# A layer norm and routing stage begun four tiles at a time, projections in token halves, and row scores by deadline

## The chip, the cores and the metric

The kernel runs on one core of one Trainium2 chip. The metric is the device time of one execution in microseconds. Before the change it is 1077.17 us, the median of 3 runs (1075.95 to 1077.93). The engines are named as the profile names them: PE (TensorE, its weight loads as PEld), DVE (VectorE), ACT (ScalarE), POOL (GpSimd) and SP (SyncE), which issues nearly all transfers. About 0.2% (2 us) is what a measurement of this kernel can tell from no change.

## The reference

`x` is 2 sequences of 1024 tokens with 128 features. Three parts follow each other: a mixture of experts, an attention, and the same mixture again.

```python
x = x + 0.5 * ffn(layernorm(x))
x = x + attn(layernorm(x))
x = x + 0.5 * ffn(layernorm(x))

def attn(x):                      # 16 heads, latent width 64, head width 8
    q = (x @ Wq + bq); k = (x @ Wk + bk); v = (x @ Wv + bv)
    qc = einsum('bthd,dl->bthl', q, Wc)
    att = softmax(causal(einsum('bthl,bshl->bhts', qc, k) / 8))
    return einsum('bhts,bshl->bthl', att, v) @ Wo + bo

def ffn(x):                       # 32 experts in 8 groups, top 4, capacity 320
    shared = silu(x @ sg) * (x @ su) @ sd
    # best 4 of 8 groups by cosine, best 4 experts among them, softmax gates,
    # each token's place within an expert by a running count, over 320 dropped
    buf = scatter(x);  h = silu(buf @ wg) * (buf @ wu);  out = h @ wd
    return shared + gathered_and_weighted(out)
```

## The kernel before, in words

The program is written engine by engine, with semaphores between them; nothing schedules it, so each engine's order is the order of the code. Tokens are 16 tiles of 128; `HT` = 8 tiles are one half, H (one sequence).

**First mixture.** `ln(0, 0)` on DVE takes the statistics of eight tiles (L847, L850), ACT the roots (L640), DVE the normalised rows (L861); PE transposes them (L1180), ACT copies them to `xnT` (L646), PE scores them against the centroids (L1188), and DVE routes them four tiles at a time (`route_steps`, from L871). When the slots of four tiles are known (L944), POOL scatters their rows to the expert buffers in HBM, one indirect transfer for each tile and choice (L552): 64 of them in a row, and the experts wait for the last. Ahead of all this DVE clears several buffers and normalises the centroids, whose transpose PE makes first (L1412). The expert loop follows, then `results` (SP, L452) loads each tile's four result rows and `combine` (DVE, L1034) adds them.

**Attention.** `ln(2, 0)` normalises the first sequence. Then four projections (`J`: q and k, each for tokens 0 to 511 and 512 to 1023; PE L1323) are split by ACT (L696, the high part) and DVE (L1046, the low part) and stored in `qkbuf` in HBM, three row blocks each (SP L476, `projected`). `group_in` loads the rows of four heads back, 4 transfers to `Qx` and 4 to `Kz`. There are 8 groups of heads (4 for each sequence), each with 4 chunks of 256 queries (a *unit*), and each unit has 4, 8, 12 or 16 *steps*: a step is one key tile for two heads. A step on PE is the transposed scores (L1356, `s_cols`), exp on ACT (L752), for the tiles on the diagonal a mask on POOL (L568), and three steps later the product with the values (L1375, `pv`).

The exp needs each row's maximum, which is added in the matmul, so the scores are computed twice. The first pass is the *row items* (`R`: PE L1331 and, on the diagonal, L1334; DVE L1052 takes the maximum). After the last `R` of a unit DVE makes the maxima ready (`max_parts`, L1061 to L1063), and a `T` item lets PE transpose them (L1342) and DVE add them to `Qx` (L1070). A unit's first step waits for its `T`. All row items use two banks in turn, so PE waits for DVE with every item but one. `ROW_STEP` says behind which step a row item stands, on PE, DVE and SP alike. In the kernel before it follows from `LEAD`: the items of a group run from step 6 of the group before it, evenly over 40 steps. There are 363 row items: 40 ahead of the first step (`EARLY`), 183 beside the 160 steps of the first sequence and 140 beside the 160 of the second, the last at step 285. The value tiles (L1290, ACT L734) of the first sequence stand between the projections and the early items.

When a unit ends, ACT copies sums (L705) and results, DVE inverts the sums (L1096), SP spreads them over the partitions with 8 transfers (L499, `spread_sums`), and POOL scales the unit (L588).

## Time and profile before

| | |
|---|---|
| median of 3 runs | 1077.17 us |
| profiled execution | 1078.49 us |
| its span | 1076.7 us |
| scatter of the first mixture, POOL | 31.8 to 112.6 us |
| expert loop | 113 to 256 us |
| from the loop's end to the first row item | 256 to 300.7 us |
| early row items | 300.7 to 328.6 us |
| steps of the first sequence, PE | 328.6 to 566 us |
| steps of the second sequence, PE | 608 to 832 us |
| second scatter, routing and second expert loop | to 1076.7 us |

The span runs from the first to the last instruction; the profiled execution's own time is 1.8 us more. A start time in a row below is counted from the beginning of the span.

### The profile page before, as it was taken

The numbers are of one execution on the slowest core, as the hardware profiler recorded it, in microseconds if no ns is written. First come the engines' busy times: TensorE is split into PE (matmuls) and PEld (weight loads), VectorE is DVE, ScalarE is ACT, GpSimd is POOL, SyncE is SP. The second block draws the span as 40 slices with busy tenths as digits, with TensorE's granted clock in tenths as the row PEclk, the third lists the DMA queues.
The fourth block names the chain that finished last, engine by engine and source line by source line (L and its number), as shares of the span: only waits on it lengthen the run. The fifth ranks groups of instructions, "written<-read, shape, count | busy, mean of one in ns | idle before, by whom it ended". The sixth has DMA issues, their size and how long they took to land.

```text
span 1076.7 us, 16412 instructions
## 1 busy us (share of the span) xinstructions
PE 873.8 (81%) x5041; PEld 720.3 (67%) x5041; DVE 567.6 (53%) x1624; ACT 406.9 (38%) x803; POOL 399.4 (37%) x583
## 2 busy tenths in 40 slices
PE   2358599992678998998999799899999845899993
PEld 1235477771246887987888488888888823687773
DVE  6743245444369665665752575566641362345444
ACT  2101132321314564554641454656566211233323
POOL 2677266654002222221210111354642046356651
PEclk9999699997789999999999899999999868899997
DMA  9510345553620011114101001112110100446536
GB/s 357 205 49 25 104 145 177 172 153 118 196 53 1 20 43 30 43 41 139 30 21 42 1 10 34 42 51 60 47 34 21 40 21 25 146 138 190 167 105 198
DMA packets 96245, 94.11 MB, mean 87 GB/s; under 512 B 15274, under 2 KB 83004, under 8 KB 95415
## 3 DMA queue, kind: packets, MB, share of 16 engines
q1 hardware_dynamic: 86966, 81.00, 25.1%
q0 software_dynamic: 9216, 12.33, 3.7%
q8 instruction: 33, 0.54, 0.2%
q14 instruction: 30, 0.24, 0.1%
HBM read 54.95 MB, written 37.03 MB: 85 GB/s over the span
## 4 chain that ended last, share of the span: by engine, by line
PE 52%; DVE 15%; POOL 10%; SPq 7%; DMA 7%; issue 7%; ACT 1%; POOLq 0%; DVEq 0%; ACTq 0%
PE PS L1375 15%; PE PS L1282 8%; POOL xbuf L552 7%; PE PS L1269 6%; SPq L499 6%; PE PS L1331 5%; PE PS L1270 5%; PE PS L1356 4%; PE PS L1406 3%; DVE mxp L1052 3%; DVE den L1096 2%; DMA rden<-den 2%; DVE xs L1034 2%; PE PS L1243 2%; POOL area_o L588 2%
## 5 line engine op out<-in xcount | busy, mean ns | idle before, releaser
L1375 PE MATMUL PS<-pT,area_v 128*128 128x256 f32 (+1 forms) x1280 | 307.7, 364 | 20.4 <-POOL pT L568 20.2
L1052 DVE TENSOR_REDUCE mxp<-PS 128x2 f32<-128x512 f32 (+1 forms) x320 | 197.7, 630 | 149.5 <-PE PS L1331 81.9
L752 ACT ACTIVATE pT<-PS 128x512 f32<-128x512 f32 (+1 forms) x320 | 176.7, 554 | 186.7 <-PE PS L1356 183.9
L1375 PEld LDWEIGHTS PS<-pT,area_v 128*128 128x128 f32 x1280 | 211.7, 192 | 36.8 <-issue 22.5
L602 POOL DMA_INDIRECT ybuf<-area_o,yidx x160 | 155.6, 973 | 128.5 <-DVE area_o L1008 89.5
L1331 PE MATMUL PS<-Kz,Qx 128*128 128x256 f32 (+1 forms) x640 | 169.0, 355 | 17.5 <-DVE mxp L1052 11.1
L552 POOL DMA_INDIRECT xbuf<-xn,sidx x128 | 125.4, 980 | 88.3 <-issue 62.0
L1356 PE MATMUL PS<-Qx,Kz 128*128 128x256 f32 (+1 forms) x640 | 142.7, 305 | 6.6 <-ACT pT L752 5.5
L1331 PEld LDWEIGHTS PS<-Kz,Qx 128*128 128x128 f32 x640 | 113.6, 196 | 39.0 <-DVE mxp L1052 19.6
L588 POOL TENSOR_TENSOR area_o<-area_o,rden 128x512 f32<-128x512 f32 x32 | 40.7, 1271 | 258.5 <-DMA rden<-den 258.5
L568 POOL TENSOR_SCALAR_AFFINE_SELECT pT<-pT 128x128 f32<-128x128 f32 x256 | 67.7, 299 | 178.9 <-ACT pT L752 178.6
L685 ACT ACTIVATE area_o<-PS 128x320 f32<-128x320 f32 x128 | 56.0, 437 | 147.0 <-PE PS L1270 138.0
L1356 PEld LDWEIGHTS PS<-Qx,Kz 128*128 128x128 f32 x640 | 102.0, 194 | 11.8 <-ACT pT L752 7.2
L1000 DVE TENSOR_TENSOR area_o<-area_o,PS 128x320 f32<-128x320 f32 x128 | 62.3, 488 | 79.2 <-ACT area_o L685 75.1
L1269 PE MATMUL PS<-area_o,area_v 128*128 128x320 f32 x256 | 96.1, 458 | 6.5 <-DVE area_o L1000 4.3
L1282 PEld LDWEIGHTS PS<-area_v,area_o 128*128 128x128 f32 x768 | 93.3, 192 | 5.3
L1282 PE MATMUL PS<-area_v,area_o 128*128 128x128 f32 x768 | 96.2, 275 | 0.0
L1270 PE MATMUL PS<-area_o,area_v 128*128 128x320 f32 x256 | 92.1, 442 | 0.0
L1096 DVE RECIPROCAL den<-den 128x128 f32<-128x128 f32 x64 | 59.4, 936 | 37.2 <-ACT den L705 37.2
L1269 PEld LDWEIGHTS PS<-area_o,area_v 128*128 128x128 f32 x256 | 44.7, 196 | 34.6 <-DVE area_o L1000 23.5
L1270 PEld LDWEIGHTS PS<-area_o,area_v 128*128 128x128 f32 x256 | 49.9, 195 | 21.3 <-issue 1.8
L705 ACT ACTIVATE den<-PS 32x256 f32<-32x256 f32 x128 | 47.9, 374 | 8.5 <-PE PS L1375 6.0
(160 smaller groups left out, 859.2 us busy)
## 6 DMA issues: line engine op xcount, KB each, us to landing
area_v<-xbuf SPq DMA_DIRECT2D x32, 340.0 KB, 3.2
area_v<-in_L_ffn_wg_dram SPq DMA_DIRECT2D x32, 256.0 KB, 3.4
area_v<-in_L_ffn_wu_dram SPq DMA_DIRECT2D x32, 256.0 KB, 3.7
area_v<-in_L_ffn_wd_dram SPq DMA_DIRECT2D x64, 128.0 KB, 2.5
rden<-den SPq DMA_DIRECT2D x256, 32.0 KB, 1.8
yg<-ybuf SPq DMA_DIRECT2D x24, 256.0 KB, 4.3
qkbuf<-stage SPq DMA_DIRECT2D x24, 256.0 KB, 3.0
xbuf<-Kz SPq DMA_DIRECT2D x4, 1360.0 KB, 10.9
```

What stands on the lines that cost most here:

```text
L552: pool.indirect_dma_start(xbuf[:, :], bass.IndirectOffsetOnAxis(ap=sidx[:, H, t * K + k:t * K + k + 1], axis=0), xn[:, H * HT + t, :], Non ...
L568: ins = nc.gpsimd.affine_select(out=block_, in_=block_, pattern=[[1, P]], compare_op=ALU.is_ge, fill=zero, base=0, channel_multiplier=-1)
L602: pool.indirect_dma_start(ybuf[:, :], bass.IndirectOffsetOnAxis(ap=yidx[:, j, t:t + 1], axis=0), yo[j][:, t, :], None, bounds_check=RES - ...
L752: nc.scalar.activation(pT[:, N % 4, 0:w], PS[:, 2 + N % 2, 0:w], ACT.Exp).then_inc(exp_done, 1)
L1052: nc.vector.tensor_reduce(mxp[:, i, c, 2 * hp:2 * hp + 2], PS[:, k % 2, 0:2 * w].rearrange("p (h w) -> p h w", h=2), AX.X, ALU.max).then_i ...
L1096: ins = nc.vector.reciprocal(part, part)
L1269: mm(PS[:, 2 + c, 0:CAP], wgt[j][:, a, c * P:(c + 1) * P], rhs, start=True, stop=True)
L1270: mm(PS[:, 4 + c, 0:CAP], wut[j][:, a, c * P:(c + 1) * P], rhs, start=True, stop=True)\
L1282: ins = mm(PS[:, bank, slot * D:(slot + 1) * D], hp[:, c, t * P:(t + 1) * P], wdt[j][:, a, c, :], start=(first and c == 0), stop=(c == HC ...
L1331: ins = mm(PS[:, k % 2, hh * w:(hh + 1) * w], Qx[Gi % 2][:, i * P:(i + 1) * P], Kz[Gi % 2][:, 2 * hp + hh, TC * c:TC * c + w], start=(hh = ...
L1356: ins = mm(PS[:, 2 + N % 2, a * w:(a + 1) * w], Kz[Gi % 2][:, 2 * p + a, j * P:(j + 1) * P], Qx[Gi % 2][:, t1 - w:t1], start=(a == 0), sto ...
L1375: ins = mm(PS[:, pv_bank(U, a), (p + 1) * TC - w:(p + 1) * TC], value_and_ones(j, h), pT[:, N % 4, a * w:(a + 1) * w], start=(first and p ...
```

## The change

It has five parts.

1. *First tiles by themselves.* The first four tiles of `x` are the first transfer, and `ln_first` does statistics, roots and normalised rows for four tiles, then the centroids (their squares now on DVE instead of ACT), then the second four tiles, and last the casts of the constants, which stood ahead of everything. PE scores tiles 0 to 3 before it transposes tiles 4 to 7. POOL clears only `Kz0` at the start and `Kz1` behind its 64 scatters.
2. *Token halves.* Combine, layer norm and transposes between the expert loop and the attention go in halves of four tiles. The projections go in the order q and k of tokens 0 to 511, then q and k of 512 to 1023. Between the halves stand four value tiles.
3. *Loads.* In `qkbuf` each head has 32 rows (8 of constants and 24 of data) instead of 26, so one transfer brings q for all four heads, and four bring k: 5 instead of 8 for a group, now called a visit. The first visit is loaded in two halves of 512 tokens. The constants are written early, behind the zeroing.
4. *Row scores by deadline.* 18 row items stand ahead of the first step, those of units 0 and 1 with the four projections. Each later visit's items end two steps before its last unit begins: 188 beside the first sequence's steps, 157 beside the second's, the last at step 301. The `T` of a visit's last unit stands directly behind that unit's last `R`, no longer three items later.
5. The second half's combine moves from steps 2 to 8 to steps 20 to 32; the 32 scatters within the second sequence stand on consecutive steps without a mask from step 210.

```diff
-R0 = 2
-RQ = R0 + 3 * HD
+R0 = RW - 3 * HD
...
+COMB_STEPS = (20, 24, 28, 32)
+SCAT_STEPS = [n for n in range(FIRST[V_C] + 10, len(STEPS)) if n not in DIAG][:K * HT]
+
...
+    for U, (vu, c) in enumerate(UNITS):
+        if vu == v:
+            pieces = [("R", i, k, min(TC, (i + 1) * P - k * TC), hp, (i, k, hp) == (2 * c + 1, c, 1))
+                      for i in (2 * c, 2 * c + 1) for k in range(c + 1) for hp in range(2)]
+            if U > 2 and UNITS[U - 1][0] == v:
+                pieces.insert(3, ("T", U - 1))
+            items += pieces
+            if U < 2 or c == VISITS[v][2][-1]:
+                items.append(("T", U))
+    if v == 0:
+        items = [("J", 0, q, h) for h in range(2) for q in range(2)] + items
...
+    if v == V_J:
+        items[14:14] = [("J", 1, q, h) for h in range(2) for q in range(2)]
...
+ROW_ITEMS = [(v, item) for v in range(len(VISITS)) for item in row_items(v)]
+ROW_NUMBER = {item if item[0] != "R" else (v, item): k for k, (v, item) in enumerate(ROW_ITEMS)}
+N_EARLY = ROW_NUMBER[("T", 1)] + 1
...
+def row_steps():
+
+    steps, end = [-1] * N_EARLY, 0
+    for v, visit in enumerate(VISITS):
+        mine = [k for k, (vk, item) in enumerate(ROW_ITEMS) if vk == v and k >= N_EARLY]
+        last = max(UNIT_FIRST[U] for U, (vu, c) in enumerate(UNITS) if vu == v) - 2
+        begin = 0 if v == 0 else max(end, FIRST[v - 1] + 3)
+        steps += [begin + i * (last - begin) // len(mine) for i in range(len(mine))]
+        end = last
...
+ROW_STEP = row_steps()
...
-EARLY = [k for k, s in enumerate(ROW_STEP) if s < 0]
...
+            def x_in_part(h):
+                sp.dma_start(xs[:, 4 * h:4 * h + 4, :], x_t[:, 4 * h:4 * h + 4, :]).then_inc(s_x[h], 16)
+
+            x_in_part(0)
             sp.dma_start(cst[:], consts).then_inc(s_const, 16)
-            for h in range(4):
-                sp.dma_start(xs[:, 4 * h:4 * h + 4, :], x_t[:, 4 * h:4 * h + 4, :]).then_inc(s_x, 16)
             sp.dma_start(cen[0:G, :], gcen).then_inc(s_cen, 16)
             sp.dma_start(cen[G:G + E, :], ecen).then_inc(s_cen, 16)
             sp.dma_start(ebb[:], ebias.partition_broadcast(P)).then_inc(s_cen, 16)
+            for h in range(1, 4):
+                x_in_part(h)
...
+            for b in range(B):
+                sp.dma_start(qkbuf[b, 0, :, 0:R0, :], Kz[0][:, 1, :].bitcast(F32)).then_inc(qk_const, 16)
+                sp.dma_start(qkbuf[b, 1, :, 2:R0, :], Kz[0][0:(R0 - 2) * NH, 1, :].bitcast(F32)).then_inc(qk_const, 16)
+                sp.dma_start(qkbuf[b, 1, :, 0:2, :],
+                             rden[0][0:4 * NH].rearrange("p a t -> p (a t)")).then_inc(qk_const, 16)
...
-            def group_in(Gi):
-
-                b, g = Gi // NG, Gi % NG
-                for j in range(2):
-                    sp.wait_ge(qk_out[j], 16 * 6 * (b + 1))
-                if Gi >= 2:
-                    sp.wait_ge(st_ready, SLOT * (Gi - 1))
+            def visit_in(v, cols, arrived):
+
+                b, g, chunks = VISITS[v]
+                heads = qkbuf[b, :, HG * g:HG * g + HG, :, cols]
+                sp.dma_start(Qx[v % 2][:, cols].bitcast(F32), heads[0].rearrange("h r t -> (h r) t")).then_inc(arrived, 16)
                 for hh in range(HG):
-                    rows = slice(RW * hh, RW * hh + RQ)
-                    sp.dma_start(Qx[Gi % 2][rows, :].bitcast(F32), qkbuf[b, 0, HG * g + hh]).then_inc(qk_in[Gi % 2], 16)
-                    sp.dma_start(Kz[Gi % 2][rows, hh, :].bitcast(F32), qkbuf[b, 1, HG * g + hh]).then_inc(qk_in[Gi % 2], 16)
+                    sp.dma_start(Kz[v % 2][RW * hh:RW * hh + RW, hh, cols].bitcast(F32), heads[1, hh]).then_inc(arrived, 16)
...
-            for k in range(4):
-                projected(k)
...
-            group_in(0)
-            group_in(1)
...
+            for h in range(2):
+                for k in range(2 * h, 2 * h + 2):
+                    projected(k)
+                if h == 0:
+                    sp.wait_ge(qk_const, 16 * 6)
+                    sp.wait_ge(s_zero1, 1)
+                    sp.wait_ge(s_fill, 64)
+                    sp.wait_ge(s_filly, 32)
+                for j in range(2):
+                    sp.wait_ge(qk_out[j], 16 * 3 * (h + 1))
+                visit_in(0, slice(512 * h, 512 * h + 512), (qk_half, qk_in[0])[h])
+            visit_in(1, slice(0, T), qk_in[1])
...
+                if step in FIRST[1:-1]:
+                    v = FIRST.index(step) + 1
...
+                    sp.wait_ge(st_ready, step)
+                    visit_in(v, slice(0, T), qk_in[v % 2])
...
+            zero_k(0, s_zero)
...
+            zero_k(1, s_zero1)
...
+            for h in range(2):
+                ln_std_dev(2, h)
+                ln_scaled(2, 0, (h,))
+                for k in range(2 * h, 2 * h + 2):
+                    high_part(k)
+                if h == 0:
+                    values(0, range(HT // 2))
+            load_table(ACT.Exp)
+            values(0, range(HT // 2, HT))
+            heads(0)
+            values(1, range(HT))
+            heads(1)
...
+            def ln_half(h):
+                ln_stats(0, *LN_FIRST[h])
+                ln_spread(2, h, *LN_FIRST[h])
+                ln_rows(2, 0, h, *LN_FIRST[h])
...
+            def ln_first():
+                dve.wait_ge(s_x[0], 16)
+                ln_stats(0, *LN_FIRST[0])
+                ln_spread(0, 0, *LN_FIRST[0])
+                ln_rows(0, 0, 0, *LN_FIRST[0])
+                centroid_squares()
+                dve.wait_ge(s_x[1], 16)
+                ln_stats(0, *LN_FIRST[1])
+                centroids()
+                ln_spread(0, 1, *LN_FIRST[1])
+                halves()
+                ln_rows(0, 0, 1, *LN_FIRST[1])
+                dve.wait_ge(s_ct, 1)
+                nc.vector.tensor_copy(cenT[:], PS[:, 6, 0:G + E]).then_inc(s_ctc, 1)
...
-                    inverses(step, b)
-                out_rows(b)
+            combine_part(0, 0, 0, 4)
+            dve.wait_ge(comb, 4)
+            ln_half(0)
+            combine_part(0, 0, 4, 4)
+            for k in range(2):
+                row_item(k)
+            dve.wait_ge(comb, HT)
+            ln_half(1)
+            for k in range(2, N_EARLY):
+                row_item(k)
...
+            for h in range(2):
+                ln_half(2, 0, h)
+                pe.wait_ge(xnT_ready, 5 + h)
+                for k in range(2 * h, 2 * h + 2):
+                    row_item(k)
+                if h == 0:
+                    for j in range(HT // 2):
+                        value_tile(0, j)
+            for i, k in enumerate(range(4, N_EARLY)):
+                row_item(k)
+                if i < HT:
+                    value_half(0, HT // 2 + i // 2, i % 2)
+            pe.wait_ge(v_a, HT)
+            pe.wait_ge(v_ones, 1)
```

Order on DVE from the first statistics on. `st`, `mv`, `rstd`, `rn` and `xn` are the layer norm, `csq` and `pT` the centroids, `yg` the routing's work space. Before:

```order
L826 TENSOR_SCALAR csq<-csq 40x1
L827 RECIPROCAL csq<-csq 40x1
L828 TENSOR_SCALAR pT<-pT,csq 40x128
L830 COPY cenT<-PS 128x40
L847 BN_STATS st<-xs 128x6 x8
L850 BN_AGGR mv<-st 128x2 x8
L853 RECIPROCAL rstd<-std 128x8
L855 TENSOR_TENSOR rn<-dev,rstd 128x8
L856 TENSOR_SCALAR rn<-rn 128x8
L857 RECIPROCAL rn<-rn 128x8
L861 TENSOR_SCALAR xn<-xs,mv,rstd 128x128 x8
```

and now:

```order
L899 BN_STATS st<-xs 128x6 x4
L904 BN_AGGR mv<-st 128x2 x4
L909 RECIPROCAL rstd<-std 128x4
L911 TENSOR_TENSOR rn<-dev,rstd 128x4
L912 TENSOR_SCALAR rn<-rn 128x4
L913 RECIPROCAL rn<-rn 128x4
L917 TENSOR_SCALAR xn<-xs,mv,rstd 128x128 x4
L867 TENSOR_TENSOR pT<-pT 40x128
L868 TENSOR_REDUCE csq<-pT 40x1
L899 BN_STATS st<-xs 128x6 x4
L872 TENSOR_SCALAR csq<-csq 40x1
```

The normalised rows of four tiles now come ahead of the centroids, which came first before.

Order on PE behind the first expert loop: transposes (`cst,xn`), projections (`xnT,wq` and `xnT,wk`), value tiles (`wv_in,xnT`) and row items (`Kz,Qx`). Before:

```order
L1180 MATMUL PS<-cst,xn 128x128 x8
L1323 MATMUL PS<-xnT,wq 128x512 x2
L1323 MATMUL PS<-xnT,wk 128x512 x2
L1290 MATMUL PS<-wv_in,xnT 128x512 x8
L1331 MATMUL PS<-Kz,Qx 128x128 x2
L1334 MATMUL PS<-causS,identb 128x256
L1331 MATMUL PS<-Kz,Qx 128x128 x2
L1334 MATMUL PS<-causS,identb 128x256
```

and now:

```order
L1259 MATMUL PS<-cst,xn 128x128 x4
L1402 MATMUL PS<-xnT,wq 128x512
L1402 MATMUL PS<-xnT,wk 128x512
L1369 MATMUL PS<-wv_in,xnT 128x512 x8
L1259 MATMUL PS<-cst,xn 128x128 x4
L1402 MATMUL PS<-xnT,wq 128x512
L1402 MATMUL PS<-xnT,wk 128x512
L1413 MATMUL PS<-Kz,Qx 128x128 x2
L1416 MATMUL PS<-causS,identb 128x256
L1369 MATMUL PS<-wv_in,xnT 128x512
L1413 MATMUL PS<-Kz,Qx 128x128 x2
L1416 MATMUL PS<-causS,identb 128x256
```

Two projections now stand behind four transposes, and four value tiles stand between the two halves.

Order on SP at the same place: result rows (`yg`), stores of the projections (`stage`) and loads. Before:

```order
L452 DMA yg<-ybuf 128x512 x16
L464 DMA qkbuf<-Kz 16x2x1024
L465 DMA qkbuf<-rden 16x4x512
L464 DMA qkbuf<-Kz 16x2x1024
L465 DMA qkbuf<-rden 16x4x512
L476 DMA qkbuf<-stage 16x8x512 x12
L488 DMA Qx<-qkbuf 26x1024
L489 DMA Kz<-qkbuf 26x1024
L488 DMA Qx<-qkbuf 26x1024
L489 DMA Kz<-qkbuf 26x1024
```

and now:

```order
L489 DMA yg<-ybuf 128x512 x16
L505 DMA qkbuf<-stage 16x8x512 x6
L512 DMA Qx<-qkbuf 128x512
L514 DMA Kz<-qkbuf 32x512 x4
L505 DMA qkbuf<-stage 16x8x512 x6
L512 DMA Qx<-qkbuf 128x512
L514 DMA Kz<-qkbuf 32x512 x4
L512 DMA Qx<-qkbuf 128x1024
L514 DMA Kz<-qkbuf 32x1024 x4
```

The first loads stand behind six stores instead of twelve, and the constants' stores are gone from here.

## Rows read from the trace of the kernel before

**Rows 1.** The page's head.

```profile
span 1076.7 us, 16412 instructions
```

**Rows 2.** Busy time by stretch: from:to, length, then each engine's, clock, DMA.

```profile
256.00:300.70 44.70, 17.59 (x33) 7.03 (x33) 16.79 (x64) 9.69 (x14) 3.22 (x1) 0.65 0.67 201
300.70:328.60 27.90, 23.58 (x102) 15.04 (x103) 21.24 (x43) 4.10 (x4) 0.00 (x0) 0.91 0.11 22
328.60:343.00 14.40, 11.69 (x79) 9.79 (x78) 14.30 (x41) 6.75 (x15) 4.94 (x16) 1.00 0.01 2
...
797.00:832.00 35.00, 33.98 (x192) 30.39 (x191) 5.29 (x6) 24.41 (x48) 9.02 (x20) 1.00 0.13 31
```

**Rows 3.** The same by stretch for the exp line L752 alone (ACT, x steps).

```profile
608.50:797.00 188.50, 70.86 (x130) 0.96 0.14 37
797.00:831.00 34.00, 17.77 (x32) 1.00 0.13 32
```

**Rows 4.** POOL in order of time: start, length, engine, line, operation [idle before].

```profile
0.81 6.96 POOL L539 MEMSET Kz<- 128x4096 f32 x2 [0.29 <-POOLq L1540]
31.76 1.11 POOL L552 DMA_INDIRECT xbuf<-xn,sidx  x1 [23.99 <-issue]
```

**Rows 5.** DVE in order of time, at the start.

```profile
5.59 0.09 DVE L818 MEMSET mxm<- 128x32 f32 x1
...
7.97 0.21 DVE L823 CAST causS<-cst 128x128 bf16<-128x128 f32 x1
...
13.11 1.63 DVE L847 BATCH_NORM_STATS2 st<-xs 128x6 f32<-128x128 f32 x8
...
15.88 0.20 DVE L853 RECIPROCAL rstd<-std 128x8 f32<-128x8 f32 x1 [0.47 <-ACT dev L641]
...
16.65 2.09 DVE L861 TENSOR_SCALAR xn<-xs,mv,rstd 128x128 f32<-128x128 f32 x8
20.90 0.19 DVE L871 TENSOR_TENSOR yg<-PS,rn 128x32 f32<-128x32 f32 x1 [2.16 <-PE PS L1188]
```

**Rows 6.** The chain that ended last, in order of time: start, length, what.

```profile
19.27 1.61 PE PS L1188 x8
...
112.86 2.18 DMA xbuf<-xn,sidx
```

**Rows 7.** DVE in order of time, behind the expert loop.

```profile
262.45 7.70 DVE L1034 SCALAR_TENSOR_TENSOR xs<-yg,gate,xs 128x128 f32<-128x128 f32 x29 [0.22 <-DMA yg<-ybuf]
...
279.88 0.75 DVE L1046 SCALAR_TENSOR_TENSOR stage<-PS,qkb,stage 128x512 fp32r<-128x512 f32 x1 [4.05 <-ACT stage L696]
...
303.18 1.36 DVE L1052 TENSOR_REDUCE mxp<-PS 128x2 f32<-128x512 f32 x2 [0.57 <-PE PS L1334]
...
305.02 0.17 DVE L1063 SCALAR_TENSOR_TENSOR M<-mxm,M 128x8 fp32r<-128x8 f32 x1
```

**Rows 8.** SP's transfers in order of time, same place.

```profile
280.66 10.56 SPq L476 DMA_DIRECT2D qkbuf<-stage  x12
...
293.70 0.33 SPq L488 DMA_DIRECT2D Qx<-qkbuf  x1
```

**Rows 9.** The chain at the same place.

```profile
283.81 4.00 DMA qkbuf<-stage
...
296.54 4.01 DMA Kz<-qkbuf
```

**Rows 10.** PE in order of time, same place.

```profile
277.04 3.78 PE L1323 MATMUL PS<-xnT,wq 128*128 128x512 f32 x4 [0.69 <-ACT xnT L646]
...
283.35 3.60 PE L1290 MATMUL PS<-wv_in,xnT 128*128 128x512 f32 x8
291.05 5.40 PE L1290 MATMUL PS<-wv_in,xnT 128*128 128x512 f32 x8 [4.10 <-ACT area_v L734]
300.69 0.66 PE L1331 MATMUL PS<-Kz,Qx 128*128 128x128 f32 x2 [4.24 <-DMA Kz<-qkbuf]
```

**Rows 11.** ACT in order of time, same place.

```profile
293.84 1.02 ACT L734 ACTIVATE area_v<-PS 128x1024 f32<-128x1024 f32 x1 [1.94 <-PE PS L1290]
```

More of the change, by code:

```diff
@@ L118 @@
-ROW_NUMBER = {item if item[0] != "R" else (Gi, item): k for k, (Gi, item) in enumerate(ROW_ITEMS)}
+    return items
+ROW_ITEMS = [(v, item) for v in range(len(VISITS)) for item in row_items(v)]
[9 more added lines that the diff above has]
+        end = last
+    for U, unit in enumerate(UNITS):
+        assert U < 2 or steps[ROW_NUMBER[("T", U)]] < UNIT_FIRST[U]
+    assert steps == sorted(steps)
+    return steps
@@ L301, in program @@
         s_dve = sem("s_dve")
[L302 removed]
+        s_csq = sem("s_csq")
         s_cn = sem("s_cn")
@@ L752, in heads @@
                     nc.scalar.activation(pT[:, N % 4, 0:w], PS[:, 2 + N % 2, 0:w], ACT.Exp).then_inc(exp_done, 1)
-                    unit_out(N, Gi // NG)
+                    unit_out(N, b)
+                for step in range(steps_of(b)[-1] + 1, steps_of(b)[-1] + 1 + DRAIN):
+                    unit_out(step, b)
             for H in range(2):
-                ln_std_dev(H)
+                if H:
+                    ln_std_dev(1)
+                else:
+                    ln_std_dev(0, 0)
+                    centroid_norm()
+                    ln_std_dev(0, 1)
                 ln_scaled(H, H)
@@ L850, in ln, with ln_stats, ln_spread @@
+            def ln_stats(H, a, b):
+                for t in range(a, b):
+                    ins = nc.vector.bn_stats(st[:, t, :], xs[:, H * HT + t, :])
+                link(ins)
+            def ln_spread(r, part, a, b):
+                for t in range(a, b):
                     ins = nc.vector.bn_aggr(mv[:, t, :], st[:, t, :])
                 ins.then_inc(ln_stat, 1)
-                dve.wait_ge(ln_std, r + 1)
-                link(nc.vector.reciprocal(rstd[:], std[:]))
-                link(tt(rn[:], dev[:], rstd[:], ALU.mult))
@@ L1399, in out_proj @@
                 n = HT * b + i
-                pe.wait_ge(norm_done, NCH * (NG * b + NG - 1) + i // 2 + 1)
+                pe.wait_ge(norm_done, max(U for U, (v, c) in enumerate(UNITS) if VISITS[v][0] == b and c == i // 2) + 1)
                 if i >= 2:
@@ L1413, in _ @@
             pe.wait_ge(s_ctc, 1)
-            ln(0, 0)
-            for f in range(2):
-                scores(f, 0)
+            scores(0, 0)
+            ln_half(0, 0, 1)
+            scores(1, 0)
+            pe.wait_ge(s_cst, 1)
             for f in range(2):
```

411 lines of the change are left out of this document (183 added, 228 removed).

## The prediction

> **What bounds the kernel now.** I read the page first, then busy time by stretch, then the chain of waits and each engine in order of time at three places. The reader is to see that no one engine bounds the whole; the span of 1076.7 us [rows 1] falls into stages with different limits. At the start POOL's 64 scatters run back to back from 31.76 us, and the chain leaves them only at 112.86 us [rows 4, 6]: 81.1 us for 64, 1.27 us each, so all that follows moves with the moment at which the first four tiles are routed. The expert loop behind it is not touched. From its end to the first row item, 256 to 300.7 us, PE is busy 17.6 of 44.7 us [rows 2]: that is a string of latencies (combine, layer norm, projections, stores, loads). The early row items, 300.7 to 328.6 us, keep DVE busy 21.2 of 27.9 us [rows 2] and PE waits for it. Then PE is the bound: with no row items left it is busy 34.0 of 35.0 us [rows 2], and 32 steps take 34 us, 1.06 us each; beside row items 130 steps took 188.5 us, 1.45 us each [rows 3].
>
> **The start.** Before, DVE ends its clearing at 5.7 us, does the casts and centroids, begins the statistics at 13.11 and the first routing operation at 20.90 us [rows 5]. Now the four-tile chain begins at 5.7, if the first part of `x` has landed. Halves of the eight-tile rows: statistics 0.82 us, aggregation (from 14.74 to 15.41, so 0.67) 0.33, the wait for ACT 0.47, reciprocal to normalised rows 0.77 (15.88 to 16.65), four rows 1.05: 9.1 us. Then on DVE, ahead of the scores, the squares of the centroids (two small operations, an estimate of 0.5), the second four's statistics 0.82, the centroids' three small operations 0.7, aggregation 0.33, the casts (0.21 each and overlapping) 0.5, the second half's 0.77 and 1.05, and the copy of the transposed centroids 0.2: 14.0 us. That copy is the gate, not the layer norm: PE can score only then. Four tiles of scores take 1.61 us [rows 6], so routing begins at about 15.9 instead of 20.9 us, with 0.2 for semaphores at 16.1. **I take 4.8 us.** Bounds: nothing, if the first scatter meets something else that is late (the zeroing of its buffer in HBM is queued behind more transfers of `x`), and 6.5 if the small operations overlap. The second four tiles have 16 scatters, 20 us, of cover for one routing of about 10 us, and the `Kz1` clearing (half of the 6.96 us in [rows 4]) stands where POOL waits for the first expert results.
>
> **From the loop to the first step.** In the times of the trace before, the shift of the start left out. The combine of 29 operations takes 7.70 us from 262.45 [rows 7], 0.27 each. For four tiles 13 are left: 266.0. Statistics, aggregation, roots, rows as above (3.4) end at 269.4, four transposes and the copy to `xnT` at 270.5; the first projections stood at 277.04 [rows 10]. Two projections at the 1.9 us each of that row: 274.3. DVE does the combine of tiles 4 to 7 first, until 273.7, then the low parts of 0.75 us [rows 7], the second one at 275.9. SP has the last result rows to issue until about 274.7 (an estimate, 1 us behind the combine), then six stores: 12 took 10.56 us with a wait among them [rows 8], I take 4 for six: 278.5; they land 4.0 behind the issue [rows 9], so near 282. Loads: 8 took from 293.70 to 300.55 [rows 8, 9]; 5 take 3 issues of 0.41 less, 5.6 us: **the first half is in SBUF at about 288**, against 300.55.
> It isn't the last thing. Behind ACT's two high parts stand four value copies of 1.02 us [rows 11], which wait for PE's value tiles of 1.8 us [rows 10]; they end near 283. Only then does ACT take the second half's roots, though DVE asks for them at 277. Then 0.47, 0.77, 1.05 us on DVE, transposes and copy, 1.5 in all: projections from 286.8. Which PE clock they get is open. The two value tiles behind a PE gap of 4.10 us took 5.40 us, the two ahead of it 3.60 [rows 10]; here the gap is about 2.7 us. At 0.95 us each the two projections end at 288.7, at 1.9 us at 290.6. The high and low parts of the second (0.7 and 0.75) follow: the first row items begin at **about 290.5**, 10 us earlier than 300.69 [rows 10]. The second half's stores and loads land near 302, ahead of the first step, which needs only the first half; its row items come behind that.
> The Trainium skill (TensorE: Matmul & The Clock Gate, What's actually happening) says that an idle PE falls to its 1.2 GHz state. By that rule alone, applied to the 2.7 us gap, the sum would be 1.9 us worse; the 4.10 us gap of [rows 10] agrees with it, for the shorter one no run here decides.
> Ahead of the first step now stand 14 row items instead of 36, with the same 8 value halves. A half costs PE 0.90 us (four in 3.60, [rows 10]), so 7.2 of the 23.58 us that PE is busy in the early stretch [rows 2]; the 36 items are the rest, 0.46 each. Now it is 7.2 + 14 x 0.46 = 13.6 us, and PE is the bound, since a half stands behind each of the first 8 items. Both `T` come directly behind an `R`: from the end of the last maximum to the end of the three maxima operations it is 0.65 us (304.54 to 305.19 in [rows 7]), then transpose and addition, an estimate of 0.4 each: 1.45 twice, 2.9. So 16.5 us: the first step at 307.0 instead of 328.7. **21.7 us.** Bounds: 10 (what the row items' begin gives, the rest lost on stalls) and 28 (the early items at no more than 27.9 x 14 / 36 = 10.9 us).
>
> **What comes back.** 22 row items are now beside the steps, 5 more in the first sequence, 17 in the second. Price from [rows 3]: (188.5 - 130 x 1.06) / 126 `R` = 0.40 us, with all other stalls of that stretch in it. I take 0.32: **+7 us** (0, if PE has slack there, to 15, if each costs DVE's 0.68 by [rows 7]).
> The `T` of each visit's last unit, directly behind its `R`, can stall PE: 1.45 us against one step of about 1.4 between. **+2** for eight (0 to 12, a whole step each). The moved combine: from 328.6 to 343 DVE was busy 14.30 of 14.4 us [rows 2], so it costs where it stands now; at steps 20 to 32 it meets 1.1 items a step instead. **+1** (-3 to +5). In visit 3 the second sequence's projections now stand in the same step as a unit's eight `spread_sums` on SP, before one step behind: **+1**. Fewer loads: nothing, SP waits for steps there and the loads have 20 steps of cover.
>
> **Sum.** -4.8 - 21.7 + 7 + 2 + 1 + 1 = -15.5. The profiled execution took 1078.49 us, 1.3 more than the median of 1077.17; so 1063 there and **1062 us** at the median (1061.7). About 0.2% is what a measurement can tell from no change.
>
> **Rivals.**
> *The second half is the gate* (0.15). ACT, DVE and SP do the two halves one behind the other, so that the row items begin near 300.7 as now, and only the 36 - 14 items are saved, 27.9 - 16.5 = 11.4 us instead of 21.7: 1072. For it: ACT's roots behind four value copies. Against: the loads of the first half need nothing of the second.
> *The moved row items are free* (0.12): the steps beside which they stand wait for masks and ACT anyway, 0 instead of +7, and the +4 of stalls fall away: 1051. Against: PE at 34.0 of 35.0 us.
> *The start gives nothing* (0.07): the scatters start when the zeroing has landed, or run slower beside the other transfers: 1067.
> *Deadlines turn into stalls* (0.06), the slower side. Each of 30 units begins with its `T` one to twelve steps behind its last `R`, no longer with the old reserve, and DVE is in order: one combine chunk, layer norm or inversion ahead of the item makes PE wait at the unit's first step. An `R`, its maxima, `T` and addition are 0.68 + 0.65 + 0.8 = 2.1 us. If PE waits a third of that at each of 30 units, 0.7 us, it is 21 us, less the 2 counted: 1081. From 0.6 us a unit on it outweighs the gain. Against: the ring of two banks makes PE wait for DVE with every item already.
>
> **Chances.** Forecast 0.60, rivals as given. Range 1050 to 1074: it holds the forecast with its bounds and the first three rivals nearly whole. Faster 0.92, within 0.2% 0.02, slower 0.06.
>
> **What would show it.** First scatter at about 27 us; first row item about 15 us and first step about 26 us earlier than now (start included); the pace at steps 288 to 304 at 1.35 us instead of 1.06; idle time of PE before the first `s_cols` of a unit small. It is wrong if the routing begins as late as before, if ACT's roots of the second half come later than 283 (less 5), or if PE waits in total more than 10 us for additions to `Qx`.

## The result and the profile after

The changed kernel takes 1081.68 us (median of 15 runs, 1075.63 to 1086.0), the kernel before 1077.09 on the same chip (15 runs, 1073.59 to 1079.43): a ratio of 1.0044, with a 95% interval of 1.0026 to 1.0062. It is slower by about 4.6 us. The forecast was 1062. Its reasons for a gain came true within 2 us, and the whole of it was lost again beside the steps. The profiled execution below took 1085.16 us, 3.5 more than the median; a second one of the same kernel (*e9*) took 1080.32 us, the median of its own runs, and stands beside it where the two differ.

The page of the profile after, its head and its busy times:

```profile
span 1083.4 us, 16405 instructions
...
PE 884.4 (82%) x5041; PEld 729.7 (67%) x5041; DVE 569.2 (53%) x1634; ACT 406.1 (37%) x804; POOL 399.0 (37%) x583
```

The start, DVE and POOL in order of time, to be laid beside [rows 4, 5]:

```profile
5.71 0.87 DVE L899 BATCH_NORM_STATS2 st<-xs 128x6 f32<-128x128 f32 x4
...
13.77 0.19 DVE L933 COPY cenT<-PS 128x40 f32<-128x40 f32 x1
15.98 0.19 DVE L941 TENSOR_TENSOR yg<-PS,rn 128x32 f32<-128x32 f32 x1 [2.02 <-PE PS L1267]
...
26.91 1.12 POOL L589 DMA_INDIRECT xbuf<-xn,sidx  x1 [22.59 <-issue]
```

The statistics begin at 5.71 instead of 13.11 us, the routing at 15.98 instead of 20.90, and the first scatter stands at 26.91 instead of 31.76: 4.85 us. The transfer of the last scatter, which the experts wait for, starts those 4.85 us earlier as well (108.01 instead of 112.86, [rows 6]; the 112.6 in the table of times ahead is a little early for it) and takes 2.2 us in both.

From the loop to the first step, all engines in order of time, for [rows 7 to 11]; 4.85 us are to be added for the times of before:

```profile
257.29 3.50 DVE L1104 SCALAR_TENSOR_TENSOR xs<-yg,gate,xs 128x128 f32<-128x128 f32 x13 [0.31 <-DMA yg<-ybuf]
...
269.59 4.84 SPq L505 DMA_DIRECT2D qkbuf<-stage  x6
...
278.29 0.29 ACT L667 ACTIVATE std<-mv,cst 128x4 f32<-128x4 f32 x1
...
278.51 0.32 SPq L512 DMA_DIRECT2D Qx<-qkbuf  x1
...
278.70 0.18 DVE L909 RECIPROCAL rstd<-std 128x4 f32<-128x4 f32 x1 [6.64 <-ACT dev L668]
...
279.78 1.10 PE L1259 MATMUL PS<-cst,xn 128*128 128x128 f32 x4 [2.45 <-DVE xn L917]
281.57 1.98 PE L1402 MATMUL PS<-xnT,wq 128*128 128x512 f32 x2 [0.69 <-ACT xnT L677]
...
285.12 0.44 PE L1413 MATMUL PS<-Kz,Qx 128*128 128x128 f32 x2
...
300.24 0.41 PE L1425 MATMUL PS<-cst,M 128*128 128x128 f32 x2 [1.54 <-DVE M L1133]
...
300.86 0.39 ACT L782 ACTIVATE pT<-PS 128x256 f32<-128x256 f32 x1 [3.82 <-PE PS L1438]
...
837.72 0.60 ACT L782 ACTIVATE pT<-PS 128x512 f32<-128x512 f32 x1 [0.50 <-PE PS L1438]
```

The first row item begins at 285.12, the first exp at 300.86 us. In the trace before the first exp begins at 329.05 and the last of the 320 at 830.07. So the first step is 28.2 us earlier, the last 7.65 us later: **the 320 steps take 536.9 us instead of 501.0.** What stands behind them takes 1 us less (245.7 instead of 246.6).

Busy time by stretch after, for [rows 2], and then the same for the exp line alone, for [rows 3]:

```profile
251.15:286.80 35.65, 19.07 (x37) 7.77 (x37) 17.50 (x69) 9.51 (x15) 2.75 (x1) 0.67 0.56 180
286.80:300.20 13.40, 10.78 (x45) 6.13 (x45) 8.54 (x19) 4.78 (x6) 0.00 (x0) 1.00 0.74 224
...
300.20:560.00 259.80, 231.42 (x1392) 207.06 (x1393) 159.56 (x326) 131.56 (x259) 51.25 (x142) 0.95 0.16 41
604.00:793.00 189.00, 172.42 (x1093) 157.21 (x1094) 119.41 (x237) 100.60 (x204) 74.49 (x155) 0.96 0.15 39
793.00:838.00 45.00, 39.24 (x223) 35.40 (x222) 16.41 (x27) 24.84 (x49) 9.02 (x21) 0.92 0.10 24
821.00:827.80 6.80, 5.22 (x19) 4.83 (x20) 1.76 (x2) 2.57 (x6) 2.91 (x9) 0.50 0.00 0
```

```profile
793.00:838.00 45.00, 17.91 (x32) 0.92 0.10 24
```

The last 32 steps took 34.0 us in [rows 3] and take 45 now. PE is idle in 5.8 us of them instead of 1.0, and for 6.8 us its granted clock is 0.50, which is 1.2 of 2.4 GHz; in the last stretch of [rows 2] it was 1.00 throughout.

The stretches of the trace before that [rows 2] doesn't have:

```profile
328.60:566.00 237.40, 218.13 (x1386) 196.67 (x1386) 156.13 (x323) 131.67 (x259) 52.62 (x143) 0.99 0.16 42
608.00:797.00 189.00, 171.83 (x1100) 157.25 (x1100) 120.62 (x244) 102.63 (x206) 74.55 (x155) 0.96 0.14 37
```

Summed over both sequences, PE was busy 423.9 of 461.4 us in these stretches and is now busy 443.1 of 493.8. They begin and end a little outside the steps; counted from the first to the last exp of each sequence PE's busy time grew from 419.6 to 441.8 us and its idle time from 37.3 to 50.9: 22 us more of work and 14 more of waiting.

What PE waited for from the first step on to the end of the steps, after and then before (line waited at, released by: us in total, times, longest):

```profile
PE PS L1455 <- POOL pT L604: 25.7, 14, 3.8
PE PS L1413 <- DVE mxp L1122: 8.9, 5, 5.2
PE PS L1438 <- ACT pT L782: 8.1, 3, 5.4
PE PS L1425 <- DVE M L1133: 5.2, 9, 1.5
...
PE PS L1413 <- DVE Qx L1140: 1.3, 1, 1.3
```

```profile
PE PS L1375 <- POOL pT L568: 20.2, 13, 2.9
PE PS L1331 <- DVE mxp L1052: 7.5, 4, 4.9
```

The largest is the wait of the value product for the masks on the diagonal. It was there before, at 20.2 us, and no row of [rows 1 to 11] names it.

### The profile page after: what moved, and what is told of

It reads as the page before. It is cut to its first block, busy times and chain, and to the rows that moved or that the text cites. A ratio compares the mean times of both kernels' runs of the same rounds, so it can differ in the third digit from the quotient of the medians.

```text
span 1083.4 us, 16405 instructions
## 1 busy us (share of the span) xinstructions
PE 884.4 (82%) x5041; PEld 729.7 (67%) x5041; DVE 569.2 (53%) x1634; ACT 406.1 (37%) x804; POOL 399.0 (37%) x583
## 4 chain that ended last, share of the span: by engine, by line
PE 52%; DVE 17%; POOL 10%; issue 7%; SPq 7%; DMA 5%; ACT 1%; POOLq 0%; DVEq 0%; ACTq 0%
PE PS L1455 15%; PE PS L1361 8%; POOL xbuf L589 7%; SPq L524 6%; PE PS L1348 5%; PE PS L1413 5%; PE PS L1349 4%; PE PS L1438 4%; DVE mxp L1122 3%; PE PS L1484 3%; DVE den L1166 3%; DMA rden<-den 2%; PE PS L1369 2%; PE PS L1322 2%; POOL area_o L621 1%
## 5 line engine op out<-in xcount | busy, mean ns | idle before, releaser
L1455 PE MATMUL PS<-pT,area_v 128*128 128x256 f32 (+1 forms) x1280 | 316.6, 372 | 25.7 <-POOL pT L604 25.7
L1455 PEld LDWEIGHTS PS<-pT,area_v 128*128 128x128 f32 x1280 | 218.3, 198 | 43.8 <-issue 28.2
L1413 PE MATMUL PS<-Kz,Qx 128*128 128x256 f32 (+1 forms) x640 | 172.5, 359 | 13.9 <-DVE mxp L1122 9.2
L621 POOL TENSOR_TENSOR area_o<-area_o,rden 128x512 f32<-128x512 f32 x32 | 40.7, 1270 | 286.8 <-DMA rden<-den 286.8
L1413 PEld LDWEIGHTS PS<-Kz,Qx 128*128 128x128 f32 x640 | 116.0, 197 | 34.6 <-DVE mxp L1122 12.3
L1438 PEld LDWEIGHTS PS<-Qx,Kz 128*128 128x128 f32 x640 | 104.4, 199 | 14.1 <-ACT pT L782 9.8
```

Source lines behind the costliest of these rows:

```text
L1413: ins = mm(PS[:, k % 2, hh * w:(hh + 1) * w], Qx[v % 2][:, i * P:(i + 1) * P], Kz[v % 2][:, 2 * hp + hh, TC * c:TC * c + w], start=(hh == ...
L1438: ins = mm(PS[:, 2 + N % 2, a * w:(a + 1) * w], Kz[v % 2][:, 2 * p + a, j * P:(j + 1) * P], Qx[v % 2][:, t1 - w:t1], start=(a == 0), stop= ...
L1455: ins = mm(PS[:, pv_bank(U, a), (p + 1) * TC - w:(p + 1) * TC], value_and_ones(j, h), pT[:, N % 4, a * w:(a + 1) * w], start=(N in UNIT_FI ...
```

## Where the masks wait

A mask is 0.25 us on POOL. But POOL is in order, and at step `SCALE_AT` (13 behind a unit's end) stands the scaling of the finished unit, which waits for its inverted sums: DVE inverts one half at step 8 and the other at step 9 (`RECIP`), SP spreads them. If they are late, the masks of the new unit, queued behind the scaling, are late too, and PE's value products wait. Here it is at unit 29, whose last exp begins at 796.81 us; DVE, POOL and PE in order of time after:

```profile
810.33 0.94 DVE L1166 RECIPROCAL den<-den 128x128 f32<-128x128 f32 x1
811.19 0.69 DVE L1122 TENSOR_REDUCE mxp<-PS 128x2 f32<-128x512 f32 x1
...
812.45 0.94 DVE L1166 RECIPROCAL den<-den 128x128 f32<-128x128 f32 x1
...
820.69 1.26 POOL L621 TENSOR_TENSOR area_o<-area_o,rden 128x512 f32<-128x512 f32 x1 [12.37 <-DMA rden<-den]
821.90 2.01 POOL L604 TENSOR_SCALAR_AFFINE_SELECT pT<-pT 128x128 f32<-128x128 f32 x8
822.58 1.19 PE L1455 MATMUL PS<-pT,area_v 128*128 128x128 f32 x4 [3.79 <-POOL pT L604]
```

and the same unit before, its last exp at 800.48:

```profile
806.74 1.76 DVE L1096 RECIPROCAL den<-den 128x128 f32<-128x128 f32 x2 [6.68 <-ACT den L705]
...
815.50 1.27 POOL L588 TENSOR_TENSOR area_o<-area_o,rden 128x512 f32<-128x512 f32 x1 [6.70 <-DMA rden<-den]
...
817.42 0.68 PE L1375 MATMUL PS<-pT,area_v 128*128 128x128 f32 x4 [0.48 <-POOL pT L568]
```

This is the widest difference of all units, since in the kernel before the last row item stood at step 285, ahead of this unit. Before, DVE had nothing else here and inverted both halves as soon as ACT had copied the sums, 6.3 us behind the last exp. Now row items stand ahead of the first inversion, and the last `R`, its maximum and the maxima operations between the two: 13.5 and 15.6 us. The scaling ends 25.1 us behind the exp instead of 16.3, eight masks of four steps run in one block behind it, and PE waits 3.79 us instead of 0.48. There is a second bill: 2.2 us into the wait, at 821.0 us, the granted clock falls to half and stays there for 6.8 us, and the products behind the wait take 1.19 us for four; at unit 29 before, four took 0.68.

The Trainium skill (PSUM — Partial Sum Buffer, Engine vs sequencer instructions) calls GpSimd's queue strictly first in, first out. The trace agrees: masks whose exp had ended stood behind the scaling's 12.37 us wait. The other rule of the Trainium skill that I had weighed (TensorE: Matmul & The Clock Gate, What's actually happening: an idle array falls to 1.2 GHz) came out at the projections: 1.9 us behind the end of the 2.45 us gap, at 281.7 us, the granted clock fell to 0.50, and the two matmuls of a projection took 1.98 us, the slower price of [rows 10]. Beside the steps the trace agrees only in part. All nine spells of half clock after begin during a PE wait of 1.5 us or more or within 2 us of its end. But of the 19 waits above 1.2 us ten have no such spell, up to one of 2.49 us. The same wait in the two executions of the changed kernel, at step 95, shows that even its length doesn't settle it: PE and then the stretch around it, first with, then (in *e9*) without the lower clock:

```profile
449.66 1.20 PE L1455 MATMUL PS<-pT,area_v 128*128 128x128 f32 x4 [3.04 <-POOL pT L604]
...
449.10:455.80 6.70, 6.14 (x25) 5.81 (x26) 1.98 (x3) 2.42 (x5) 3.16 (x9) 0.50 0.10 25
```

```profile
448.79 0.68 PE L1455 MATMUL PS<-pT,area_v 128*128 128x128 f32 x4 [3.02 <-POOL pT L604]
...
448.30:455.00 6.70, 6.21 (x42) 5.82 (x43) 3.36 (x5) 4.11 (x8) 3.09 (x9) 1.00 0.10 25
```

PE is equally busy in both, with 25 matmuls at half clock and 42 at full: half clock costs some 0.4 of the time that PE is busy in it.

The records of the granted clock hold 17.1 us at half within the steps before, and 47.8 after (34.1 in *e9*).

## The experiments

Every kernel but one is derived from the changed one. Runs of a group share the runs of the kernel before. In the second group everything, the kernel before too (1143.4 us), took some 6% longer, so of that group only ratios within it are used; the third repeats what matters of it.

**Group 1** (kernel before 1076.07 us).

*e1_old_rows.* The row order of before, `T` three items behind, 40 early items, the early combine, and the second sequence's projections at steps 102 to 105 instead of 113 to 116:

```diff
-            if U > 2 and UNITS[U - 1][0] == v:
+            if U:
...
-            if U < 2 or c == VISITS[v][2][-1]:
+            if U == len(UNITS) - 1:
...
-ROW_STEP = row_steps()
+ROW_STEP = [40 * (v - 1) + LEAD + k * 40 // len(row_items(v)) for v in range(len(VISITS)) for k in range(len(row_items(v)))]
+N_EARLY = sum(s < 0 for s in ROW_STEP)
```

> The changed kernel with the row items' old order and steps (40 ahead of the first step, the T three items behind its unit's last R, combine at steps 2 to 8); the earlier start, the token halves and the new loads stay. Theory S (the deadline schedule lost the gain: PE stalls beside the steps, each followed by a spell at the low clock): the first step comes about 15 us earlier than in the kernel before (near 314 us), the 320 steps take as long as there, and the time is 1058 to 1067 us, ratio to before 0.983 to 0.991. Rival R (what the steps lost comes from something else in the change, the 32-row loads or the halves): the steps stay some 30 us longer and the time is over 1072 us.

1065.24 us, ratio 0.9902 (0.9868 to 0.9936). First exp at 317.01, steps of 501.2 us, waits for masks 19.5 us. So the start, the halves and the loads gain 11 us, and the row order, with the places of combine and projections that go with it, costs about 16. The first step comes 12 us earlier than in the kernel before and not the 15 expected.

*e2_scale_later.* The scaling four steps later. A unit's masks stand on its first four steps, so in the two units of each visit whose masks stood right behind a scaling they now stand ahead of it (the drain behind a sequence is four steps longer to hold it):

```diff
-EVAC, RECIP, SCALE_AT, DRAIN = LAG + 1, LAG + 5, LAG + 10, 16
+EVAC, RECIP, SCALE_AT, DRAIN = LAG + 1, LAG + 5, LAG + 14, 20
```

> The changed kernel with POOL's scaling of a unit 17 steps behind its end instead of 13. Theory P (a good part of the loss is POOL waiting in order for the spread sums while the next unit's masks stand behind it): PE's waits for masks (25.7 us in all in the changed kernel) fall under 6 us, low-clock spells beside the steps become fewer, and the time falls by 12 to 25 us, to 1057 to 1070. Theory S without P: the masks come earlier but PE then waits for row items instead, under 5 us gained, 1077 or more.

1042.84 us, ratio 0.9692 (0.9659 to 0.9725): 39 us for one place in the order, far more than the 12 to 25 expected. POOL in order of time at unit 29:

```profile
782.75 0.54 POOL L604 TENSOR_SCALAR_AFFINE_SELECT pT<-pT 128x128 f32<-128x128 f32 x2 [0.56 <-ACT pT L782]
783.64 1.27 POOL L621 TENSOR_TENSOR area_o<-area_o,rden 128x512 f32<-128x512 f32 x1 [0.34 <-DMA rden<-den]
```

The masks come first, and the scaling waits only 0.34 us for its sums. PE waits for no mask in this trace, and the clock is at half for 19.9 us of the steps instead of 47.8.

*e3_combine_early.* `COMB_STEPS` back at 2, 4, 6, 8:

> The changed kernel with the second half's combine back at steps 2, 4, 6 and 8 (it was moved to 20 to 32). If the move is what costs (stalls of 1.3 to 1.7 us at steps 22, 27 and 35 and a low-clock spell at 343 us): 4 to 8 us less, 1074 to 1078. If DVE is as full at the early steps (11 row items in 8 steps): within 2 us of the changed kernel's 1081.7.

1083.43 us, ratio 1.0065 (1.0044 to 1.0087): its interval overlaps that of the changed kernel. The place of the combine costs nothing that can be measured.

*e4_before_scale_later.* The kernel before, with the edit of e2:

> The kernel before with POOL's scaling of a unit 17 steps behind its end instead of 13. Theory P: its 20.2 us of PE waiting for masks fall under 6 us, and the time falls by 12 to 18 us, 1059 to 1065. If the masks are not the limit but stand beside another wait: under 5 us.

1055.0 us, ratio 0.9795 (0.9761 to 0.9829), again more than expected, steps of 478.8 us and no wait for masks. With masks out of the way in both, the whole change gains 12.2 us (1055.0 to 1042.84); with them in the way it loses 4.6. The same change has opposite signs by one constant that it doesn't touch.

**Group 2.**

*e5_inversions_together.* Both inversions of a unit at step 8:

```diff
-                    for U in units_at(step, RECIP + half, b):
+                    for U in units_at(step, RECIP, b):
```

> The changed kernel with DVE's two inversions of a unit's sums in one step (8 behind the unit's end) instead of steps 8 and 9; scaling stays at 13. Theory Q (what makes the masks later than in the kernel before is the second inversion standing behind the visit's last row item and its maxima, 2.1 us behind the first instead of 1.3): SP's spread of the second unit of each visit starts 2 us earlier, PE's waits for masks fall from 25.7 to under 15 us, and the time falls to 1058 to 1070. If the masks' lateness comes from elsewhere (SP's eight transfers, ACT's sums): under 4 us gained, 1077 or more.

Ratio 0.9911 (0.9885 to 0.9938), as theory Q expected. Waits for masks 11.1 us.

*e6_deadline_earlier.* The deadline six steps ahead of a visit's last unit instead of two, the second projections four items later:

```diff
-        items[14:14] = [("J", 1, q, h) for h in range(2) for q in range(2)]
+        items[18:18] = [("J", 1, q, h) for h in range(2) for q in range(2)]
...
-        last = max(UNIT_FIRST[U] for U, (vu, c) in enumerate(UNITS) if vu == v) - 2
+        last = max(UNIT_FIRST[U] for U, (vu, c) in enumerate(UNITS) if vu == v) - 6
```

> The changed kernel with every visit's row items ending 6 steps ahead of its last unit instead of 2, so that the last R, its maxima and the T stand at step 17 of a visit and not at 20 and 21, between the inversions; scaling at 13, the second sequence's projections still from step 113. Theory Q: waits for masks fall to under 20 us, time 1068 to 1076. Theory that a late T itself is what costs (PE waits at unit starts): the waits for maxima fall instead, by the 5 us they are. If the density of items does it: no change, 1079 to 1084, since it stays 1.1 a step and rises in the first visit.

Ratio 0.9993 (0.9963 to 1.0022), waits for masks 23.3 us. The waits did not fall under 20 us, so the last `R` and its `T` alone, moved from between the inversions, are not what makes most of the lateness: other row items still stand there. Whether the time fell a little against 1.0044 stays open, since the changed kernel itself was not in this group and two edits are in it.

*e7_scale_later_j_moved.* e2 with the second projections at `items[5:5]`:

> The changed kernel with the scaling 17 steps behind a unit's end (1042.8 alone) and the second sequence's projections from step 106 instead of 113, between two units' spreads on SP. If the projections' stall (5.5 us at step 115, and a low-clock spell of 6.8 us behind it) comes from their stores standing behind eight spread transfers: 4 to 8 us less, 1035 to 1039. If it is the two stage buffers and the stores' landing alone: within 2 us of 1043.

Ratio 0.9781 (0.9727 to 0.9834).

*e8_old_rows_scale_later.* e1 with the edit of e2:

> The old order and steps of the row items (1065.2) with the scaling at 17. With the masks off the path the deadline order should be worth what the prediction said of it, fewer early items against more beside the steps: if so this is slower than the deadline order's 1042.8 by 2 to 6 us, 1044 to 1049. If the deadline order loses even then, this is faster: 1042 or less.

Ratio 0.9788 (0.9735 to 0.9842). The two can't be told apart here and were run again.

**Group 3** (kernel before 1075.25 us; the kernels are the changed one and those of e5, e8 and e7).

> The changed kernel itself, as the reference of this group, since in the group before it all times were 6% longer. Both theories expect its first ratio again, 1.0044 of the kernel before (1.0026 to 1.0062); on an undisturbed chip 1081 to 1083 us, steps of 537 us, about 26 us of waits for masks.

1080.32 us, ratio 1.0047 (1.0031 to 1.0063): the result stands on its own. In this execution the steps took 532.7 us with 34.1 us at half clock and 27.1 us of waits for masks, in the first 536.9 with 47.8 and 25.7.

> The changed kernel with both inversions of a unit in one step. Theory (masks): the work between the two inversions is what delays the scaling, and so the masks queued behind it on POOL; waits for masks go from 26 to about 11 us as in the first look, the low-clock spells go with them, the steps take about 521 us instead of 537 and the time is 1066 us (ratio to before 0.990, to the changed kernel 0.985). Rival (deadline stalls: the additions to Qx and the maxima are what PE waits for): moving an inversion ahead of the last row items only makes them later, so the time stays at 1082 us or rises to 1085.

1064.56 us, ratio 0.9904 (0.9882 to 0.9926): 15.8 us are back, as the theory of the masks expected (1066), and against its rival (1082 to 1085), although the `T` waits grew from 3.7 to 9.8 us. The steps took 514.5 us with 20.2 at half clock, in an execution of 1060.76 us, below its median. The largest waits of PE in it:

```profile
PE PS L1455 <- POOL pT L604: 10.6, 8, 2.0
PE PS L1425 <- DVE M L1133: 9.8, 8, 1.4
```

and unit 29, last exp at 777.19, DVE, POOL and PE:

```profile
790.40 1.75 DVE L1166 RECIPROCAL den<-den 128x128 f32<-128x128 f32 x2
...
799.72 1.26 POOL L621 TENSOR_TENSOR area_o<-area_o,rden 128x512 f32<-128x512 f32 x1 [11.52 <-DMA rden<-den]
...
801.62 0.68 PE L1455 MATMUL PS<-pT,area_v 128*128 128x128 f32 x4 [2.00 <-POOL pT L604]
```

The second inversion ends 15.0 us behind the last exp instead of 16.6, PE waits 2.00 instead of 3.79 us, and its clock does not fall: four products in 0.68 us. The first inversion stands behind row items as before (13.2 us), so part of the wait stays.

> The changed kernel with the old row order, the early combine and the scaling four steps later: what is left of the change is the start, the halves and the loads, with masks never behind a scaling. Against the kernel before with the scaling four steps later (1055.0 us, 0.9795) it should have the 4.85 us of the start and the 7.2 us of the halves less: 1043 us, 0.969. If that is so, the deadline order gives nothing of its own even with the masks out of the way, since the changed kernel with the later scaling was 1042.8. Rival (the deadline order gains its earlier first step, 16 us, and loses only part of it): this kernel is 5 to 10 us slower than 1042.8, so 1048 to 1053.

1043.6 us, ratio 0.9707 (0.9686 to 0.9729), as expected of the deadline order giving nothing of its own: e2 with that order had 0.9692 (0.9659 to 0.9725), 1042.84 us. Busy time by stretch, first of this kernel, then of e2:

```profile
317.50:545.00 227.50, 219.89 (x1386) 199.81 (x1385) 155.25 (x323) 131.19 (x259) 53.82 (x143) 0.97 0.18 46
587.70:797.50 209.80, 201.43 (x1276) 183.78 (x1277) 124.23 (x246) 125.59 (x252) 84.50 (x175) 0.98 0.15 40
```

```profile
299.80:538.00 238.20, 224.29 (x1401) 201.66 (x1400) 158.58 (x327) 131.36 (x259) 52.77 (x143) 0.97 0.17 44
580.00:796.00 216.00, 206.28 (x1318) 188.24 (x1318) 135.72 (x267) 125.97 (x253) 84.83 (x175) 0.98 0.15 39
```

> The changed kernel with the scaling four steps later and the four projections of the second sequence nine row items earlier in their visit. If the 5 us stall at these projections is given back and the items that now come behind them pay nothing: 1038 us, ratio 0.965, and the fastest of all. If the stall only moves to another item: 1042 to 1043 us.

1040.28 us, ratio 0.9675 (0.9652 to 0.9698): the fastest median of all, 35.0 us under the kernel before. It lies between the two expectations (1038 and 1042 to 1043): the stall of 5.5 us in e2 has become two of 2.9 and 1.2. Its interval overlaps that of e2, so that it beats e2 is likely and not shown. Steps 96 to 127 take 50.9 us in its trace instead of 54.7 in e2. Against e11, in the same group, it is 3.3 us faster, and each of its five runs (1037.83 to 1041.56) is faster than each of e11's (1042.5 to 1045.01). So with the projections better placed the deadline order is worth some 3 us of its own; in group 2 the same two kernels differed by 1.3 us (e7, e8), within their intervals.

The kernels that cross the row order with the place of the scaling, with the kernel before ahead of them. The times are medians. All else is from the traces, in us: steps from the first exp to the last, idle time of PE from the first to the last exp of each sequence:

| row order, scaling | first exp | steps | PE idle in the steps | half clock | time |
|---|---|---|---|---|---|
| before (old, 13; old start) | 329.0 | 501.0 | 37.3 | 17.1 | 1077.1 |
| old, 13 (e1) | 317.0 | 501.2 | 37.2 | 19.6 | 1065.2 |
| old, 17 (e11) | 317.9 | 478.9 | 16.0 | 21.5 | 1043.6 |
| deadline, 13 (after) | 300.9 | 536.9 | 50.9 | 47.8 | 1081.7 |
| deadline, 17 (e2) | 300.4 | 494.5 | 23.6 | 19.9 | 1042.8 |

Masks in the way cost 22 us of steps in the old order and 42 in the new one (38 in the second execution of it).

## Why the prediction was wrong

**The start: right.** 4.8 us forecast, 4.85 measured; the routing at 15.98 us for 15.9 to 16.1. A little of that is luck: the parts named in the prediction (the copy's end at 14.0, 1.61 of scores, 0.2 for semaphores) add up to 15.8, and from the copy's end to the routing it took 2.0 us and not 1.8. That the copy of the centroids' transpose is late and not the layer norm was right as well, though it ended at 13.96 instead of 14.0 with other small operations overlapped than I had assumed.

**From the loop to the first step: right, 1.7 us more than forecast.** With the shift of the start taken out, the combine of the first half ended at 265.6 (forecast 266.0), the stores were issued by 279.3 (278.5), ACT's second roots began at 283.1 (near 283), the second projections at 286.4 (286.8), the first row item at 290.0 (290.5). The first exp moved by 28.2 us in all, 26.5 were forecast. The open clock question went to the slower level. It was made up by the first row item, which began right behind the projections at 285.12 us and did not wait for their high and low parts, 1.45 us in the forecast. From the first row item to PE's first step it took 15.3 us for 16.5.

But e1 shows what this is worth. With the 40 early items left in place, the first exp is only 12.0 us earlier, 4.85 of it by the start. The other 16.2 us came from moving 22 row items from ahead of the steps to beside them, and that is a gain only if they are cheaper there.

**"What comes back": this is the step that failed.** I gave it 7 + 2 + 1 + 1 = 11 us. It was 35.9 (31.7 in the second execution), and it failed twice.

*The 22 items, mis-sized.* With masks out of the way the steps take 15.6 us longer in the deadline order (494.5 to 478.9), not 7. In the second sequence the price was right: 17 items, 5.6 us (214.8 to 209.1), 0.33 each against 0.32 taken. In the first, 5 items came with 9.9 us: PE waits 5.5 us in one piece behind the four projections in e2, 2.4 in e11, and three times for DVE at steps 22 to 35, 3.6 us in all, where e11 has one wait of 1.3 at step 6. From the first to the last exp of each sequence 8.0 us of it are PE work and 7.6 idle time. The work is 0.36 us for each of the 22 items, against the 0.46 that the prediction read for one ahead of the steps, so there was little slack to hide them in. 2.1 of the 15.6 us are the place of the projections (steps of 492.5 us in e12). Ahead of the first step the items had cost 16.2 us (e1) or 17.6 (e11); beside them 15.6. That is why e2 and e11 have about the same time.

*The masks, left out of the sum.* I priced what DVE does for PE directly, and not what stands behind DVE on SP and POOL. The maxima that moved late in a visit now surround the inversions. Over the eight second units of a visit the second inversion begins 16.2 us behind the last exp, 14.3 before, and the scaling ends at 25.3, 23.1 before, while the first masked step comes only 1.4 us later. Unit 29 weighs much in these means: over the other seven the scaling ends at 25.3 instead of 24.1, and the masked step comes 0.8 later. Waits for masks grew by 5.5 us only, 3.3 of them at unit 29. Shown: with the scaling moved, 42 us of steps are back instead of 22 (e2, e1 and e11), and with the inversions side by side half of them (e10). What part the lower clock has is an estimate, made in two ways. The two executions of the changed kernel differ by 13.7 us at half clock and 4.2 us of steps, some 0.3 us per us: 9 us for the 30.7 us more than before. And PE was busy in 40.4 us of the half clock instead of 12.1; at 0.4 of that, from the matmuls counted at step 95, it is 11. With 15.6 for the items and 5.5 for the waits it makes 30 to 32 of the 35.9. PE's idle time is accounted for by it (7.6 and 5.5 of the 13.6 us more); the 4 to 6 us that stay open are in its busy time.

**The direct `T`, the combine, the spread.** Waits at `T` (L1425) are 5.2 us from 300 us on, 1.5 of them ahead of the first step: 3.7 us beside the steps where it was 0.4 before (L1342), 2 more forecast. The combine: 1 forecast, none measured (e3). The projections, in the same step as the spreading: 1 forecast; PE's wait behind them is 5.4 us, where before it was 2.5 and 1.5.

**The rivals.** *Deadlines turn into stalls* had the size, 1081, by luck, and not the mechanism. PE waited 1.3 us for an addition to `Qx`, not 21, and 5.2 for the maxima; what I named as the sign of my being wrong (more than 10 us of waits for `Qx`) did not appear. My list of signs had no entry for POOL at all. *The second half is the gate*: no, the first row item came as forecast. *The moved items are free* was the furthest from what happened. The pace at steps 288 to 303, which I gave as 1.35 us a step, was 1.39, and 1.05 before; it was from step 304 to the last, where no row item stands, that 1.48 instead of 1.10 (1.08 in e2) showed the masks.

**The range.** It was 1050 to 1074. The bounds of the items' term (0 to 15) and of `T` (0 to 12) were in the text; together at their ends they would have made 1080. I drew the range as if at most one could go wrong, and a chain that ends on POOL had no bound in it at all, though the page before had a line for PE's waits for masks, the largest of its waits beside the steps.

## What to carry to other kernels

Work taken off the front of a pipeline and put beside it pays only if the price beside it is lower; here some 17 us became 15.6, and 13.5 with the projections placed better (e12), so the early start was worth little. When instructions are moved on an engine that runs in order, follow what it feeds two queues further: DVE's inversions, SP's spreading, POOL's scaling, and the masks that only share a queue with it. And before a large reordering, look at the longest entry in the list of waits of the stage that you reorder: here one constant (the scaling four steps later) was worth 21 us in the old kernel and 39 in the new.

## What the runs showed that I had not expected

- A stall can be paid twice. At unit 29 the clock fell to the lower of its two levels within a wait of 3.79 us and stayed there for 6.8 us, four value products in 1.19 instead of 0.68 us; behind a wait of 2.00 us, in e10, the clock stayed up. What decides it no run here shows: at step 95 it fell at a wait of 3.04 us in one execution of the changed kernel and not at one of 3.02 us in another. Over the steps these two had 47.8 and 34.1 us at half clock.
- Half clock costs less than half: 25 matmuls instead of 42 in 6.7 us of nearly full work, and 13.7 us more of it came with steps 4.2 us longer. All are from two profiled executions, so this is an estimate.
- The place of the scaling moves no work (POOL's busy time is 399.0 and 401.5 us) and is worth more (21 us in the kernel before) than all five parts of the change (12 us with the masks out of the way).
